# Second edge loop of a two-layer graph network: one signal of TensorE per pair of groups, four PSUM banks, base products two pairs behind

## The reference, cut to what matters

```python
h = jnp.maximum(_layernorm(x, axis=-1), 0.0)
W = (w_comp @ weight.reshape(B, I * O)).reshape(R, I, O)      # R = 8, B = 4
proj = jnp.einsum('ni,rio->nro', h, W)
msg = proj[src, rel_type]
agg = jax.ops.segment_sum(msg, dst, num_segments=h.shape[0])
x = x + relu(h @ root_weight + agg + bias)
```

## Time and profile before

| | |
|---|---|
| median of the runs | 10822.45 us |
| the profiled execution, its own time | 10715.39 us |
| its span (first to last instruction) | 10713.5 us |
| second edge loop, first gather issued to last gather issued | 5563.3 to 10653.7 us |
| mean granted TensorE clock | 0.738 of full |
| busy share of the span: PE, PEld, DVE, ACT, POOL | 64%, 47%, 39%, 9%, 58% |
| HBM traffic, mean over the span | 60 GB/s |

### The profile page before, as it was taken

One profiled execution on the slowest core, in us unless ns is written; L12 is line 12 of the kernel. 1 busy time (PEld: TensorE's weight loads), 2 busy tenths in 40 slices (PEclk: granted clock), 3 DMA queues, 4 the chain that ended last, 5 costly groups with the idle time before them and its releaser, 6 DMA issues. The chain is left out here.

```text
span 10713.5 us, 121075 instructions
## 1 busy us (share of the span) xinstructions
PE 6851.7 (64%) x29274; PEld 5007.3 (47%) x29274; DVE 4179.3 (39%) x8208; ACT 972.0 (9%) x1807; POOL 6253.1 (58%) x6283
## 2 busy tenths in 40 slices
PE   5777777677777677776775555555555555555555
PEld 4444444444444444444444445444444444444544
DVE  4444444444444444444452333333333333333333
ACT  2001011011010010011120000000000000000001
POOL 3555555555555555555526666666666666666664
PEclk7777777777777777777786677777777777777677
DMA  5222222222222222222231111111111111111112
GB/s 148 73 75 73 74 73 74 71 74 74 74 74 73 73 74 72 73 74 73 72 85 40 39 40 42 40 40 40 40 40 40 40 41 40 38 43 40 40 42 56
DMA packets 424873, 644.68 MB, mean 60 GB/s; under 512 B 128466, under 2 KB 244890, under 8 KB 424196
## 3 DMA queue, kind: packets, MB, share of 16 engines
q0 software_dynamic: 200704, 411.44, 14.0%
q1 hardware_dynamic: 211348, 226.21, 7.1%
q10 hardware_dynamic: 12768, 6.42, 0.2%
HBM read 615.44 MB, written 28.13 MB: 60 GB/s over the span
## 5 line engine op out<-in xcount | busy, mean ns | idle before, releaser
L543 POOL DMA_INDIRECT G<-p_tab,idxs x3136 | 2985.9, 952 | 2329.8 <-DVE idxs L650 1348.9
L1082 POOL DMA_INDIRECT hT<-h_tab,idxs x3136 | 3265.9, 1041 | 1842.8 <-issue 907.8
L1099 PE MATMUL psA<-S,hT 128*128 128x256 f32 x6272 | 2082.9, 490 | 1796.6 <-issue 894.1
L1099 PEld LDWEIGHTS psA<-S,hT 128*128 128x128 f32 x6272 | 1455.5, 244 | 2115.8 <-issue 1082.4
L667 DVE TENSOR_TENSOR_SCAN R<-mk,R,psM 128x512 f32<-128x512 bf16 x784 | 998.2, 1273 | 1687.0 <-issue 785.5
L581 PE MATMUL psM<-Z,w 128*128 128x512 f32 x1568 | 1129.6, 811 | 816.0 <-ACT Z L638 724.1
L1179 DVE TENSOR_TENSOR aggT<-psV,aggT 128x64 f32 x784 | 175.7, 224 | 3290.4 <-remote 1949.4
L597 PE MATMUL psE<-E,O 128*128 128x64 f32 x6272 | 1038.1, 322 | 429.9 <-DVE E L678 314.5
L1109 PEld LDWEIGHTS psV<-A,V 128*128 128x128 f32 x6272 | 1001.1, 230 | 583.2 <-ACT A L1127 300.1
L1109 PE MATMUL psV<-A,V 128*128 128x64 f32 x6272 | 964.3, 307 | 448.4 <-ACT A L1127 257.1
L597 PEld LDWEIGHTS psE<-E,O 128*128 128x128 f32 x6272 | 989.4, 240 | 502.5 <-DVE E L678 354.1
(11 more groups left out here) (84 smaller groups left out, 2520.9 us busy)
## 6 DMA issues: line engine op xcount, KB each, us to landing
mk<-marks SPq DMA_DIRECT2D x392, 256.0 KB
G<-p_tab,idxs POOLq DMA_INDIRECT x3136
pl<-marks SPq DMA_DIRECT2D x392, 128.0 KB
hT<-h_tab,idxs POOLq DMA_INDIRECT x3136
Qw<-q_tab SPq DMA_DIRECT2D x784, 32.0 KB
xa<-in_x SPq DMA_DIRECT2D x14, 448.0 KB, 5.0
p_tab<-pr SPq DMA_DIRECT2D x14, 448.0 KB, 3.3
oh<-in_w SPq DMA_DIRECT2D x392, 4.0 KB
```

Source lines behind the costliest of these rows:

```text
L543: pool.indirect_dma_start(G[:, s, j, :], None, p_tab, bass.IndirectOffsetOnAxis(ap=idxs[:, s, j:j + 1], axis=0)).then_inc(gathered[s], 16)
L1082: pool.indirect_dma_start(G[:, s, j, :], None, h2_tab, bass.IndirectOffsetOnAxis(ap=idxs[:, s, j:j + 1], axis=0)).then_inc(l1_gathered[s], 16)
L1099: ins = nc.tensor.matmul(psA[:, b, 0:NB * W], G[:, s, j, :], S[:, b, j, :, :].rearrange("p b w -> p (b w)"), start=j == 0, stop=j == GT - 1)
```

## The change

Only the second edge loop is changed. Two groups become one pair (1024 edges); all engines step by pairs.

- PE sends one signal a pair, pair_done, behind the last matmul of the step. A step is the sums of pair p (eight matmuls of 256 columns as before, for both halves u = 0, 1, into the two halves of one bank) and then the base products of pair p-2 (4 matmuls of 128 columns where there were 8 of 64). summed and based are gone. PE waits for the S of each half on its own.
- psA and psV have four banks each where they had two; PE's wait for a free bank looks four pairs back.
- ACT copies 512 columns once a pair and waits for pair_done alone. A has two buffers of a pair.
- DVE makes hot for both groups in one operation (128x512), S in two operations as before, each with its own signal, and waits ahead of hot, where it used to wait ahead of S, for the PE step two pairs back. The adds (still one a group, each with its register read) are three pairs behind and wait for pair_done of the step that holds the base products.
- S moves into the buffer hT behind the gather slots; it has the size of two pairs, twice what it was.
- POOL waits per pair (8 gathers) for pair_done of eight pairs back; row numbers are still copied for 4 groups at a time and 8 groups ahead (LEAD = 4 and QUAD = 2 pairs).

```diff
-LEAD = 8
-QUAD = 4
+LEAD = 4
+PPL = GPL // 2
+QUAD = 2
+BANKS = 4
...
-                            if there(k - GPL):
-                                pool.wait_ge(summed, k - GPL + 1)
+                            if there(p - PPL):
+                                pool.wait_ge(pair_done, p - PPL + 1)
...
+                        def sums(i, q):
+
+                            p, b = PPL * i + q, q % BANKS
+                            if there(p - BANKS):
+                                pe.wait_ge(sums_copied, p - BANKS + 1)
+                            pe.wait_ge(l1_gathered[q], 16 * 2 * GT * (i + 1))
+                            for u in range(2):
+                                pe.wait_ge(sel_ready, 2 * p + u + 1)
+                                for j in range(GT):
+                                    ins = nc.tensor.matmul(psA[:, b, u * NB * W:(u + 1) * NB * W], G[:, 2 * q + u, j, :],
+                                                           S[:, q % 2, u * GT + j, :, :].rearrange("p b w -> p (b w)"),
+                                                           start=u + j == 0, stop=u * GT + j == 2 * GT - 1)
+                            return ins
+
+                        def bases(p, b):
+                            pe.wait_ge(sums_copied, p + 1)
+                            if there(p - BANKS):
+                                pe.wait_ge(l1_added, 2 * (p - BANKS) + 2)
...
+                        def step(i, q):
+                            p = PPL * i + q
+                            ins = sums(i, q)
+                            if there(p - 2):
+                                ins = bases(p - 2, (q + BANKS - 2) % BANKS)
+                            ins.then_inc(pair_done, 1)
...
+                        def step(i, q):
+                            p = PPL * i + q
+                            act.wait_ge(pair_done, p + 1)
+                            nc.scalar.activation(A[:, q % 2, :, :, :].rearrange("p u b w -> p (u b w)"), psA[:, q % BANKS, :],
                                                  ACT.Copy).then_inc(sums_copied, 1)
...
+                        def select(i, q):
+                            p = PPL * i + q
+                            if there(p - 2):
+                                dve.wait_ge(pair_done, p - 1)
...
+                        def add(p, b):
+                            dve.wait_ge(pair_done, p + 3)
+                            for u in range(2):
+                                k = 2 * p + u
+                                after(dve, l1_added, k)
```

More of the change, by code:

```diff
@@ L9 @@
 TPI = GT * GPI
+PPI = GPI // 2
 AHEAD = 5
@@ L1013, in gnn @@
         l1_idx_ready = sem("l1_idx_ready")
-        l1_gathered = [sem(f"l1_gathered{n}") for n in range(GPL)]
+        l1_gathered = [sem(f"l1_gathered{n}") for n in range(PPL)]
         types_hot = sem("types_hot")
@@ L1030, in sum_edges @@
                 L1I = NGRP // GPL
[L1031 to L1032 removed]
+                GN, SN = GPL * GT * D, 2 * 2 * GT * NB * W
+                assert NGRP % GPL == 0 and L1I >= 3 and GN + SN <= NT * P
+                G = hT[:, 0:GN].rearrange("p (s j d) -> p s j d", s=GPL, j=GT)
+                S = hT[:, GN:GN + SN].rearrange("p (c t b w) -> p c t b w", c=2, t=2 * GT, b=NB)
                 def rounds(eng, step):
[L1036 to L1037 removed]
+                    for q in range(PPL):
+                        step(0, q)
                     with eng.Fori(1, L1I - 1) as i:
[L1039 to L1042, removed]
+                        for q in range(PPL):
+                            step(i, q)
+                    for q in range(PPL):
+                        step(L1I - 1, q)
                 typ = sb("typ", [P, ET], i32)
@@ L1089, in _ @@
                         pe.wait_ge(l1_consts, 16 * (NB + 3))
[L1091 to L1107, removed]
-                            for n in range(NB):
[L1109 to L1116, removed]
+                        def sums(i, q):
[5 more added lines that the diff above has]
+                                pe.wait_ge(sel_ready, 2 * p + u + 1)
+                                for j in range(GT):
+                                    ins = nc.tensor.matmul(psA[:, b, u * NB * W:(u + 1) * NB * W], G[:, 2 * q + u, j, :],
+                                                           S[:, q % 2, u * GT + j, :, :].rearrange("p b w -> p (b w)"),
+                                                           start=u + j == 0, stop=u * GT + j == 2 * GT - 1)
+                            return ins
@@ L1173, in add @@
-                        def add(k, b):
-                            dve.wait_ge(based, k + 1)
-                            after(dve, l1_added, k)
-                            dve.nop(nofuse=True)
-                            r0 = dve.value_load(win[0:1, bass.ds(k, 1)], min_val=0, max_val=NP)
-                            to = aggT[:, bass.ds(r0, W)]
-                            nc.vector.tensor_tensor(to, psV[:, b, 0:W], to, ALU.add).then_inc(l1_added, 1)
-                        for s in range(0, LEAD, QUAD):
-                            indices(0, s)
@@ new lines, in add @@
+                        def add(p, b):
+                            dve.wait_ge(pair_done, p + 3)
+                            for u in range(2):
+                                k = 2 * p + u
+                                after(dve, l1_added, k)
+                                dve.nop(nofuse=True)
+                                r0 = dve.value_load(win[0:1, bass.ds(k, 1)], min_val=0, max_val=NP)
+                                to = aggT[:, bass.ds(r0, W)]
+                                nc.vector.tensor_tensor(to, psV[:, b, u * W:(u + 1) * W], to, ALU.add).then_inc(l1_added, 1)
@@ new lines, in _, with step @@
+                        for q in range(0, LEAD, QUAD):
+                            indices(0, q)
+                        def step(i, q):
+                            p = PPL * i + q
+                            if q % QUAD == 0 and not (isinstance(p, int) and p + LEAD >= NPAIR):
+                                indices(i + (q + LEAD) // PPL, (q + LEAD) % PPL)
+                            if q % PPI == 0:
+                                coefs(2 * i + q // PPI)
+                            select(i, q)
+                            if there(p - 3):
+                                add(p - 3, (q + BANKS - 3) % BANKS)
```

94 lines of the change are left out of this document (40 added, 54 removed).

## The result

The changed kernel takes 10650.13 us (median of four runs, 10643.95 to 10663.44), the kernel before 10821.01 us beside it: a ratio of 0.9848, 95% interval 0.9821 to 0.9874. It is faster by 1.5%, 171 us. The forecast was 10,050 us, with 9870 as the low and 10,330 as the high end. The direction was right and the size was off by more than four times.

The account below looks back on a forecast made before the run. It took POOL, stopped by TensorE signals late beside its gathers, as the bound. Waits gone -880, longer gathers +67, residual stops +40, tail +5 make -768 us: 10822 - 768 = 10,054, rounded to 10,050 us; range 9870 to 10,330.

Parts of the forecast that it names:

- What bounds the kernel now: Second edge loop: POOL is stopped by TensorE signals late beside its gathers, about 1.84 us each, 3.68 us a group.
- PE sends 392 signals in place of 1568. At 1.84 us each, the lateness of a pair falls from 7.36 to 1.84 us.: TensorE's signals in the second edge loop: fewer signals cut lateness, making POOL the bound at 10.8 us a pair.
- first rival: TensorE's lateness goes with time or work, not signal count; gain 200 to 600 us: 14 in 100; no change: 3.
- middle case: TensorE at 5.5 us a signal, two-step overlap lost: 11.6 us a pair, gain 560 us, total 10,260 us.
- Its waits of 931.0 us go: POOL's waits for slots and row numbers in the second edge loop vanish, worth 880 us after its usual gaps.
- POOL's lengthening, +67 us: POOL's gathers lengthen beside other engines' work if POOL never rests: cost 67 us, bounds 0 and 301 x 2.
- The DVE, PE and ACT edits are worth 0, up to 392 us if POOL were not the bound.: Engine work per pair fits inside POOL's 10.8 us: worth 0, otherwise up to 1 us a pair, 392 us.
- Waits added: DVE's wait ahead of hot bears 7 us of lateness, POOL's later slot costs nothing; the tail adds 5 us.
- The rule of a price per increment: Semaphore increments serialize at about 26 ns each: 1176 fewer signals give 31 us; the prediction held rows 4 contradict it.
- The second rule, a full block of POOL by S: POOL can't write descriptors while DVE's S holds their shared port pair; as a rival 10,606 us, 4 in 100.

Follow-up runs that it names:

- e3: Changed kernel with the gathers of three of every four tiles left out: 7882.73 us, 0.7287 of the kernel before.
- e4: Changed kernel with POOL's 8 gathers a pair issued as plain in-order loads of the same size from SP: 7892.37 us, 0.7296 of the kernel before.
- e2: Changed kernel with two more TensorE signals a pair, for which nobody waits: 10671.10 us, 0.9861 of the kernel before.
- e1: Changed kernel with base products as eight matmuls of 64 columns a pair again, still one signal: 10888.57 us, 1.0063 of the kernel before.
- e10: Changed kernel with TensorE waiting for its own previous signal ahead of each step: 8445.77 us (0.9849 of before); on another chip 10757.46 us (0.9956).
- e12: Changed kernel with row numbers copied 12 groups ahead in place of 8: 10369.73 us (0.9609 of before); on another chip 8484.96 us (0.9905).
- e7: Changed kernel with sums signalled and copied per group, base products one pair behind: 10449.81 us (0.9724 of before); on another chip 10552.19 us (0.9770).
- e6: Changed kernel with 16 empty TensorE instructions a pair between sums and base products: 10449.18 us, 0.9734 of the kernel before.
- e11: Changed kernel with 16 empty TensorE instructions ahead of each pair's sums: 8455.13 us, 0.9858 of the kernel before.

## Why the prediction was wrong, by its own steps

- *What bounds the kernel now.* Right where it was measured: POOL is stopped by late TensorE signals, and they are late beside POOL's gathers (e3, e4). What the trace could not show is that this is so on some chips only.
- *The step that failed: "PE sends 392 signals in place of 1568. At 1.84 us each, the lateness of a pair falls from 7.36 to 1.84 us."* I divided lateness by signals because signals were what the rows showed late, and so made it a price of each signal. It stayed as it was: 4988.3/392 = 12.7 us a pair, less the 4.35 us of the loop's end, is 8.4 us, not 1.84. Two signals a pair more cost nothing (e2), and one signal a pair with narrow products gains nothing (e1). The time goes with TensorE's loads and products: 16 of them a pair are worth 238 us (e1). In outcome this is the prediction's first rival, lateness by time or work, which has 13.1 us a pair for no gain. I gave it 17 in 100, and reasoned it away with the steady beat of POOL, which says nothing about TensorE. (Its middle case is also added up wrongly: 5.7 + 5.5 is 11.2 us a pair, not 11.6.) Why a signal is late stays open; what the runs show is that it needs no load or product behind or between (e10) and that most of the late time ends after POOL has stopped.
- *"Its waits of 931.0 us go".* They became 960.0 us. Where no signal is late they are 19.3 us (16.6 + 2.7), so the term was right in kind for a bound that was never reached where signals are late.
- *POOL's lengthening, +67 us.* The sign was wrong: 1041 to 991 ns, a gain of 159 us in the profiled execution. What shortened the gathers against the kernel before was not tried. Among the changed kernels they are longer where POOL rests less, as the prediction had it: 990 ns with 963 us of stops, 1016 with 454 (e12).
- *"The DVE, PE and ACT edits are worth 0, up to 392 us if POOL were not the bound."* The base products, put down here, were the whole gain where signals are late (e1).
- *"Waits added".* Costed at nothing; the coarser steps with all else but the products cost 64 us (e1 against before), and finer steps gave back 91 (e7).
- *The rule of a price per increment* (the Trainium skill, "TensorE: Matmul & The Clock Gate", section "The cost: per-tile semaphore tail") would make the 1176 signals an estimated 31 us. I set it aside because signals were 4 us late. That was no argument: signals can be late and their number cost nothing. e2 is in agreement with the page and not with me: two more signals a pair changed the ratio by 0.0013, within the intervals.
- *The second rule, a full block of POOL by S:* no run shows it; the gathers became shorter. The prediction took the rule too far besides. The Trainium skill, "SBUF — State Buffer", section "Who interferes with whom", reports that a tensor_tensor, which S is, was not seen to stall DMAs. The gather beside S is in agreement with that.

The range was too narrow because the middle ground of the first rival was priced at a gain of 200 us at the least, where its honest lower end was zero; the measured 171 lies in that gap. That the direction came out right is partly luck: the gain came from an edit that the prediction put at nothing.

## What to carry to other kernels

When an engine's signals come late, don't divide the lateness by their number: an average is not a price. An extra signal that nobody waits for, and the same signals with more instructions between them, tell in two runs which of the two has one. Then look whether the signal is still late when its sender has nothing else to do, before you call the instructions its cause. Where one engine starves another, more buffered lead (here row numbers 12 groups ahead, 0.961 of before) can gain more than fewer messages. And repeat a comparison on another chip: the ratio may hold while the cause behind it doesn't exist there.

## What the runs showed of the hardware that I had not expected

- Beside POOL's gathers TensorE's signals come late, by 30.3 us with no load or product of its own in between (e10), on three chips of five in the experiments; on the other two none does in the traces kept (mean 0.04 us for the changed kernel), and the kernel before takes 8570 us in place of 10,735 to 10,825.
- On those three chips the changed kernel, and those near it, also have stretches in which TensorE's loads and products start 0.70 us apart or twice that. In the profile after, some fifty such stretches are 10 us long or more. When TensorE waits for its own signal ahead of each step there are none (e10), and in the kernel before none either.
- Plain loads of the same size from SP do not have this effect on a chip where gathers do (e4), nor does a quarter of the gathers (e3).
- In the changed kernel the first ten products of a step run without a gap even beside such a stretch. That this is what the queue holds is a guess: in e1 gaps begin earlier in a step, and in e10 all 24 products run without one.
- Empty instructions in TensorE's stream, 16 a pair, cost nothing that shows (e6), and 12 us on a chip without late signals (e11).
